# Graph attention layer on one core: feed-forward jobs of four row tiles, a pool of four PSUM banks, and a new order of steps

## The reference

```python
q, k, v = [(h @ W).reshape(n, 8, 64) for W in (Wq, Wk, Wv)]
e = einsum('ehd,ehd->eh', k[src], q[dst]) / sqrt(64)
ex = exp(e - segment_max(e, dst)[dst])
attn = ex / segment_sum(ex, dst)[dst]
a = segment_sum(attn[:, :, None] * v[src], dst).reshape(n, 512)
x1 = layernorm(h + a @ Wo, ln1_g, ln1_b)
f = relu(x1 @ W1 + b1) @ W2 + b2          # 512 -> 64 -> 512
layer = layernorm(x1 + f, ln2_g, ln2_b)
out = layernorm_plain(x + layer)          # no gain, no bias
```

## Time and profile before

| what | us |
|---|---|
| three runs | 682.5, 683.04, 686.41 |
| median | 683.04 |
| the profiled execution, first to last instruction (its span) | 682.0 |
| PE busy in it | 641.5 (94%) |
| DVE, ACT, POOL busy | 578.0, 528.3, 401.7 |

### The profile page before, as it was taken

One profiled execution on the slowest core, in us unless ns is written; L12 is line 12 of the kernel. 1 busy time (PEld: TensorE's weight loads), 2 busy tenths in 40 slices (PEclk: granted clock), 3 DMA queues, 4 the chain that ended last, 5 costly groups with the idle time before them and its releaser, 6 DMA issues. The chain is left out here.

```text
span 682.0 us, 10864 instructions
## 1 busy us (share of the span) xinstructions
PE 641.5 (94%) x3520; PEld 483.8 (71%) x3520; DVE 578.0 (85%) x1391; ACT 528.3 (77%) x1140; POOL 401.7 (59%) x363
## 2 busy tenths in 40 slices
PE   5999999999999999999999999999999999999950
PEld 2778877777777777777777777777778778675520
DVE  7668769879898898898889889988989898899792
ACT  2525269877888987988798889878878999698881
POOL 7267244867675865756776574864547726735423
PEclk9999999999999999999999999999999999999995
DMA  7844154644643745674474456455554824536452
GB/s 227 220 101 133 44 123 106 173 122 142 148 121 131 159 121 148 167 157 92 146 177 117 113 161 137 105 168 123 127 128 155 184 62 135 139 77 138 131 113 91
DMA packets 37747, 91.44 MB, mean 134 GB/s; under 512 B 8346, under 2 KB 9642, under 8 KB 37690
## 3 DMA queue, kind: packets, MB, share of 16 engines
q0 software_dynamic: 31536, 82.74, 47.6%
q1 hardware_dynamic: 6154, 8.01, 4.3%
HBM read 71.20 MB, written 20.99 MB: 135 GB/s over the span
## 5 line engine op out<-in xcount | busy, mean ns | idle before, releaser
L558 ACT ACTIVATE squares<-rows,nmean 125x512 bf16<-125x512 f32 x200 | 142.3, 713 | 41.5 <-DVE nmean L902 19.8
L412 POOL DMA_INDIRECT x_rows<-in_x_dram,node_idx x40 | 48.2, 1205 | 56.8 <-DVE rows L917 47.3
L416 POOL DMA_INDIRECT out_dram<-rows,node_idx x40 | 46.4, 1160 | 56.4 <-ACT rows L618 47.0
L473 POOL DMA_DIRECT2D x_rows<-in_L_gnn_ln_b_dram x40 | 52.9, 1372 | 31.1 <-DVE rows L821 21.7
L898 DVE SCALAR_TENSOR_TENSOR rows<-pF,rows 125x512 f32<-125x512 f32 x78 | 50.6, 686 | 23.2 <-PE pF L1103 22.5
L963 PE MATMUL pP<-wo_hi,aT_hi 128*125 128x512 f32 x160 | 65.9, 412 | 0.3 <-DVE aT_lo L848 0.3
L963 PE MATMUL pP<-xTs_hi,wv_hi 128*128 128x500 f32 x160 | 65.8, 411 | 0.0
L963 PE MATMUL pP<-xTd_hi,wq_hi 128*128 128x500 f32 x160 | 65.4, 409 | 0.1
L963 PE MATMUL pP<-xTs_hi,wk_hi 128*128 128x500 f32 x160 | 63.5, 397 | 0.6 <-ACT q L539 0.6
L963 PE MATMUL pP<-wo_lo,aT_hi 128*125 128x512 f32 x160 | 63.1, 394 | 0.0
L963 PE MATMUL pP<-wo_hi,aT_lo 128*125 128x512 f32 x160 | 63.0, 394 | 0.0
(11 more groups left out here) (197 smaller groups left out, 1760.6 us busy)
## 6 DMA issues: line engine op xcount, KB each, us to landing
x_rows<-in_L_gnn_ln_b_dram POOLq DMA_DIRECT2D x40, 512.0 KB, 6.7
dst_row<-in_dst_dram SPq DMA_DIRECT2D x9, 250.5 KB
q<-in_L_gnn_Wq_dram SPq DMA_DIRECT2D x1, 1024.0 KB, 5.6
rows<-in_L_gnn_Wk_dram SPq DMA_DIRECT2D x1, 1024.0 KB, 7.8
rows<-in_L_gnn_Wv_dram SPq DMA_DIRECT2D x1, 1024.0 KB, 6.8
x_rows<-in_L_gnn_Wo_dram SPq DMA_DIRECT2D x8, 128.0 KB, 6.0
xd<-in_x_dram,dst_idx POOLq DMA_INDIRECT x40, 4.6
xs<-in_x_dram,src_idx POOLq DMA_INDIRECT x40, 3.8
```

Of the source, the lines that this page charges most:

```text
L412: pool.indirect_dma_start(rows, None, x, bass.IndirectOffsetOnAxis(ap=table[:, column:column + 1].bitcast(U32), axis=0), bounds_check=N - ...
L416: pool.indirect_dma_start(out, bass.IndirectOffsetOnAxis(ap=table[:, column:column + 1].bitcast(U32), axis=0), rows, None, bounds_check=N ...
L473: pool.dma_start(xr_wide[n], bass.AP(tensor=be2.tensor, offset=be2.offset, ap=[[0, P], [0, 2], [1, D]]), accum_op=ALU.add).then_inc(s[f"be ...
L558: ins = act.activation(squares[:, t, :], w[n][:, t, :], ACT.Square, bias=nmean[c][n][:, t:t + 1], accum_out=sq[c][n][:, t:t + 1])
```

## The change

1. **PSUM.** Four banks pF hold only F2, row tile t in pF[t % 4]. Four banks pB hold everything else: the transposes, T, S, Q, K, V, O and F1. A string of digits, BANKS, gives each such step in PE's order its bank, and a step waits until the reader of the bank's last tenant has read it (`bank_free`, which now knows eight kinds of tenant).
2. **Feed-forward jobs of four tiles.** N0 with N1, and E0 with E1, share F1, relu and the small operations (m1, r1, m2, r2, m3, r3 and the square roots d1 to d3) in rounds 0 to 8; in round 9 each slot is a job of its own (SPLIT_FROM). F1 is eight matmuls of 250 columns, relu one operation of 128x250, F2 four matmuls. T becomes two steps T0 and T1 of four transposes. F1 starts its own accumulation, so the clearing by ACT is gone; each slot's two banks are seeded by ACT in one step. The special steps of the end (T9, B9, F19, F29, norm9, z9) are gone.
3. **Start.** The destination row alone is cast and transposed first (CASTD, TURND) and written to its table (TABD); then the other two. POOL's iotas for the counting (IOTB) move behind the first gathers. The Wk load waits for xd, the Wv load for xs. The low half of Wq moves ahead of the digits, three counting groups behind Q0.
4. **Destination row.** `dst_row` now shares its memory with `weight`, so the row of the next round is loaded only when the logarithm of this round has been taken.
5. **Order.** The table has an explicit time for every step in every round. FILLERS has 53 matmuls instead of 58, 24 of them ahead of O0 of round 9.

The core of the diff:

```diff
-PERIOD = 7684
-SLOT_PERIOD = {"N0": 7687, "N1": 7689}
+SPLIT_FROM = {"N": 9, "E": 9}
 PLAN = {
...
-V0 27356 105501 136738 136738 170605; O0 89451 141151 143013 157654 247834; TXD1 -186065 -14365 126120 126712 125690;
...
+TURND 279; TURN 562; OFFS 717; TURNF 866; TXD1 1194 3244 7938 13356 20768 25683 34085 38033 44554 49682; TXD0 1237 3602 7531
...
+BANKS = """
+012301230230231023102310231023102312301231023102310231023102120123021302102132013130123012301230123012302103021320132013201320123
...
+    (0, "TXD1"): 10, (0, "Q0"): 3, (9, "O0"): 24, (9, "E0.F1"): 4, (9, "E1.T0"): 4, (9, "E1.F1"): 8
...
+        pF = [ctx.enter_context(nc.psum_tensor(f"pF{n}", [P, 512], F32)) for n in range(4)]
+        pB = [ctx.enter_context(nc.psum_tensor(f"pB{n}", [P, 512], F32)) for n in range(4)]
...
+            on.wait_ge("xd_loaded", 64)
+            sp.dma_start(stage["k"], Wk.rearrange("(k p) n -> p k n", p=P)).then_inc(s["wk_loaded"], 16)
...
             for i in range(1, ROUNDS):
                 on.wait_ge("mask_eq", i)
+                on.wait_ge("log_taken", i)
                 sp.dma_start(dst_row[:, :], bass.AP(tensor=dst.tensor, offset=dst.offset + (EG * i - 1), ap=[[0, P], [1, EG + 1]]))\
...
+                    elif what == "seed":
+                        h = int(job[1])
...
+                        for t in (2 * h, 2 * h + 1):
+                            ins = act.activation(pF[t][0:R, :], bias_all[0:R, :], ACT.Copy)
...
+            def bank_free(i, step):
...
+                j, old = tenant_before[i, step]
+                if old[:3] in ("TXD", "TXS"):
+                    on.wait_ge("xd_lo" if old[2] == "D" else "xs_lo", nth("dve", old, j))
+                elif old[0] == "Q":
+                    on.wait_ge("q_saved", nth("act", old, j))
+                elif old[0] == "K":
+                    on.wait_ge("qk_part", nth("dve", old, j))
+                elif old == "S":
+                    on.wait_ge("weight_exp", j + 1)
+                elif old[0] == "V":
+                    on.wait_ge("weighted", nth("dve", f"W{old[1]}", j))
+                elif old[0] == "O":
+                    on.wait_ge("hx_done", nth("dve", f"H{old[1]}", j))
+                elif old.endswith(".F1"):
+                    on.wait_ge("h_done", nth("act", old.replace("F1", "relu"), j))
+                else:
+                    on.wait_ge("nT_done", nth("act", old, j))
...
                     elif what == "F1":
...
                         for k in range(KC):
-                            for t in range(2):
-                                ins = pe.matmul(pF[0][DFF * t:DFF * t + DFF, 0:R], w1[:, k, :], nT[:, k, R * t:R * t + R],
-                                                start=False, stop=(k == KC - 1), skip_group_check=True)
+                            by_half = nT[:, k, :].rearrange("p (h c r) -> p c h r", h=2, c=2)
+                            for c in range(2):
+                                ins = pe.matmul(bank[DFF * c:DFF * c + DFF, span(job)].rearrange("p (h r) -> p h r", r=R), w1[:, k, :],
+                                                by_half[:, c, halves(job)[0]:halves(job)[-1] + 1, :], start=(k == 0), stop=(k == KC - 1))
...
                     elif what == "F2":
...
-                        for t in range(2):
-                            pe.matmul(pF[1 - t][0:R, :], hT[DFF * t:DFF * t + DFF, :], w2[DFF * t:DFF * t + DFF, :],
-                                      start=False, stop=True, skip_group_check=True).then_inc(s["f_filled"], 1)
+                        for h in halves(job):
+                            for c in range(2):
+                                pe.matmul(pF[2 * h + c][0:R, :], hT[DFF * c:DFF * c + DFF, R * h:R * h + R], w2[DFF * c:DFF * c + DFF, :],
+                                          start=False, stop=True, skip_group_check=True).then_inc(s["f_filled"], 1)
```

More of the change, by code:

```diff
@@ L291, in graph_attention @@
-        turns = [(i, step, half) for i, step in pe_steps if step[:2] == "TX" or step.endswith((".T", ".T9"))
-                 for half in range(1 if step[:2] == "TX" else 2)]
-        turn = {key: n for n, key in enumerate(turns)}
-        products = [(i, step) for i, step in pe_steps if "." not in step and step[0] in "QKVO" and step[1:].isdigit()]
-        place = {key: n for n, key in enumerate(products)}
-        jobs = [(i, step.split(".")[0]) for i, step in pe_steps if step.endswith((".F1", ".F19"))]
@@ L330, in nth, with last_of @@
[L330 to L331 removed]
+            for i, step in steps[engine]:
+                done[family(step)] = done.get(family(step), 0) + (len(halves(step.split(".")[0])) if "." in step else 1)
+                numbers[engine, step, i] = done[family(step)]
+        def nth(engine, step, i):
+            return numbers[engine, step, i] if i >= 0 else 0
+        def last_of(engine, prefix, i):
+            return max(nth(engine, f"{prefix}{k}", i) for k in range(4))
@@ new lines, in graph_attention, with job_before, span, columns @@
+        jobs = [(i, step.split(".")[0]) for i, step in steps["pe"] if step.endswith(".F1")]
+        def job_before(i, job, h):
+            earlier = [old for old in jobs[:jobs.index((i, job))] if h in halves(old[1])]
+            return earlier[-1] if earlier else None
+        def span(job):
+            return slice(R * halves(job)[0], R * (halves(job)[-1] + 1))
+        def columns(job):
+            first = 4 if job[0] == "E" else 0
+            return slice(first + 2 * halves(job)[0], first + 2 * halves(job)[-1] + 2)
@@ new lines, in _ @@
+                    job, what = step.split(".")
+                    if what in ("T0", "T1"):
+                        e = int(what[1])
+                        on.wait_ge("n1_done", nth("act", f"{job}.norm", i))
+                        for c in range(2):
+                            for n, t in enumerate(rows_of(job)):
+                                ins = pe.transpose(bank[:, 2 * R * c + R * n:2 * R * c + R * n + R],
+                                                   w_rows[:, t, P * (2 * e + c):P * (2 * e + c) + P], ident[0:R, 0:R])
+                        ins.then_inc(s["turned"], 1)
```

821 lines of the change are left out of this document (367 added, 454 removed).

## The result

The changed kernel takes 706.98 us (median of four runs, 705.19 to 711.05), the kernel before beside it on the same chip 684.18. The ratio is 1.035, interval 1.033 to 1.038. The forecast was 666.6. The profiled execution has a span of 705.4 against 682.0.

The account below looks back on a forecast made before the run. The prediction took PE, 94% busy, to bound the kernel. Start -3.5, changes of kind -7.5, wider product -1, bank waits +1.8, round 9 hole 0, tail -6.2 summed to -16.4: 666.6 us, with 656 to 683 for 8 in 10.

Parts of the forecast that it names:

- the sum's steady stretch: Rounds 1 to 9 without their ends: saved ACT and DVE work beside PE gains nothing; bank waits add 1.8 us.
- rival H: From the experiments: the remaining mid-run idle time is ACT and DVE order around the norm, or the four shared banks.
- theory E: From the experiments: POOL's queue is bound by its order; issues pile up behind the stall, delaying scatters and node gathers.
- The zero for the destination row: Each round's later destination-row load costs 0; wholly uncovered, up to 6.7 us a round.
- Rival B: Pool of four banks starves PE at K-T-S-V and TX groups: 29 us of waits, about 694; chance 0.08 with B2.
- The sign set for B: PE idling over 2 us a round before a transpose, S or V with a DVE or ACT releaser.
- Rival B2: Gaps of 3 us a round lower PE's clock in the steady stretch: some 700 us; chance 0.08 with B.
- Changes of kind: On PE, fewer entries into products and feed-forward products from another kind: -7.5 us, from -5 to -9.
- the wider product: F1 of four-tile jobs, eight matmuls on 250 columns instead of twice eight on 125: -1 us, from 0 to -3.3.
- The start's marker: First xd gather at about 4.1 us and Q0 at 16 to 17.5; the start's term was -3.5, from -5 to 0.
- what the prediction called the risk: At the start, ACT's in-order weight splits could make K0 pay for the delayed Wk load; term's bound 0.
- The tail's marker: Last O to last row in 23 to 27 us; the tail's term was -6.2, from 0 to -12.4.

Follow-up runs that it names:

- e5: Changed kernel with POOL's four list gathers of rounds 3 to 9 moved ahead of its stall; 691.80 us, 1.011 of the kernel before.
- e7: Changed kernel with four unused iotas on POOL ahead of each round's list gathers, 15.1 us in all; 725.08 us, 1.059 of the kernel before.
- e9: The kernel before with the same four unused POOL iotas a round as e7; 683.84 us, ratio 1.0006.
- e6: e5 with the source gathers of rounds 3 to 9 moved behind the edge scatters and node gathers; 727.33 us, 1.064 of the kernel before.
- e8: e6 with SP asking for Wk at once behind Wq; 727.15 us, 1.063 of the kernel before.
- e10: Changed kernel with the weight splits of V and O moved behind work that doesn't wait for their loads; 714.29 us, 1.045 of the kernel before.
- e11: e5 with the moved weight splits of e10; 691.73 us, 1.013 of the kernel before.
- e13: Changed kernel with one bias addition for a job's four tiles instead of two, rounds 0 to 8; 713.23 us, 1.044 of the kernel before.
- e15: e14 with the joint bias additions of e13; 689.64 us, 1.009 of the kernel before.
- e16: e5 with the edits of e10, e3 and e13 (moved splits, Wk first, joint bias additions); 693.51 us, 1.015 of the kernel before.
- e2: Changed kernel with two-tile jobs in all rounds, first edge slot's steps earlier, a pair's F1 sharing a bank; 725.34 us, 1.059 of the kernel before.
- e14: e5 with e3's edit (list gathers in the stall, Wk behind Wq), without moved splits; 685.37 us, 1.003 of the kernel before.
- e3: Changed kernel with SP asking for Wk right behind Wq, without waiting for xd; 706.24 us, 1.033 of the kernel before.
- e4: Changed kernel with eleven constant matmuls ahead of the first edge transposes of rounds 1 to 5; 705.55 us, 1.033 of the kernel before.

## Why the prediction was wrong

**The step that failed is the sum's steady stretch.** The prediction asked there which engines lie beside PE, named DVE and ACT, and took their saved work as "slack for the new order's waits"; the waits it weighed were for banks (+1.8) and for the destination row (0). POOL stood in the same row with 343 of 561 us and was asked only about the start. The step to take would have been: POOL issues 32 DMAs a round at about 1.3 us each, some 42 of 62 us, in order; where in the new order does it stand, and what is queued behind? The count above (31 issues in 43 us behind stalls of 11 and 6) is what was missing. PE's idle time in the middle rose by 22.2 us against the 1.8 in the sum. e5, e7 and e9 show POOL's part: the same kernel takes 15 us less, with 12.7 us less idle time of PE in the middle, by the place of 28 issues; 15 us of POOL work cost 18, and cost nothing in the kernel before. So some 13 of the 22 are shown to be POOL's order; the other 9 stay open (rival H), and the forecasts from theory E failed in e6, e8, e10, e11, e13, e15 and e16. Why the new table leaves the stall there (jobs of four tiles finish more rows at once, or only the table's times) isn't separated; e2 says that narrow jobs in the new order keep it. The zero for the destination row held on DVE: from round 1 on it is never idle for more than 0.02 us before the mask that reads the row. In rounds 2 and 7, though, the mask starts 0.02 us behind the row's landing (127.4 and 455.4 us) and could not have stood earlier, and POOL waits for it there (14.7 and 10.6 us): whether the shared memory forced a late place of the mask on the table is not tested.

**Rival B** named the right sign, and came nearest to the height (694), but mostly by another mechanism, so by luck. In the changed kernel the waits for a bank's reader are 7.0 of the 25.0 us, far under its 29; 2.3 of them are for an H that itself waited 3.0 for a scatter. They are also four times the 1.8 of the sum. The sign set for B, over 2 us a round before a transpose, S or V with DVE or ACT as releaser, shows (14.5 + 2.3 + 0.8 + 1.2 in eight rounds), but most of it is T waiting for the norm and not for a bank: the sign didn't tell the two apart. Rival B2's mechanism came as a companion: gaps of 2.4 to 3.3 us, and 0.83 of the full clock in the 10 us behind one. The Trainium skill, TensorE: Matmul & The Clock Gate, A second HAM failure mode: psum-queue depth-cycling, tells of a kernel in which cycling through PSUM banks left PE briefly idle so often that its clock swung. Here the rings of four banks cycle through 100 to 600 us at a mean of 1.00 in e14 and 0.99 in the changed kernel, and the falls there are those behind the four gaps.

**Changes of kind and the wider product came out in the size forecast; two other parts of PE's work were not in these terms.** -7.5 and -1 were forecast. Counted from each matmul's start to the next, idle time left out, products, F1 and F2 take 7.7 us less in the changed kernel, 6.3 in e5 and 9.5 in e14. PE's work as a whole is 3.1, 8.0 and 9.9 less, and that these agree with 8.5 in e5 and e14 is in part luck. The bias matmuls of round 9 are gone in all three, 5.5 us:

```profile
L1072 PE MATMUL pF<-bias_all,ident 125*125 125x512 f32 x8 | 3.9, 605 | 0.0
...
L1072 PE MATMUL pP<-bias_all,ident 125*125 125x512 f32 x4 | 1.9, 593 | 0.0
```

(The lines count each to its own end.) Against this, the transposes take 8.4 us more in the changed kernel, 3.8 in e5 and 4.9 in e14; in the changed kernel those of T, which stand first behind the gaps, come every 0.125 us instead of every 0.110. A full F1 took 1.85 us, as forecast (1.8 to 2.0):

```profile
61.29 1.92 PE L1069 MATMUL pB<-nT,w 128*64 128x250 f32 x16
63.14 0.50 PE L967 MATMUL pB<-xTs_hi,wv_hi 128*128 128x500 f32 x1
```

Inside this run a pair of records starts every 0.212 us, 106 ns a record; 1.85 / 16 is 116 because the first pair takes 0.266 and the last one 0.309 until the product behind it. The prediction's 62 and 265 ns hold the ends of their runs in the same way: inside the runs, a record of 125 columns takes 53 ns in the kernel before, one of 512 takes 215 in the changed kernel. The Trainium skill's rule that the prediction set against its rows (TensorE: Matmul & The Clock Gate, Back-to-back issue gap) gives 55, 107 and 216, so the trace agrees with it inside a run, and the prediction was wrong to see the 512 columns against it. The -5 worked out from it was still too much: F1 as a whole takes 3.0 us less, since the ends of the runs stay.

**The start's marker was right, its term wrong.** The first gather issues at 4.61 (forecast 4.1) and Q0 starts at 16.34 (16 to 17.5), 4.6 earlier than the earlier trace rows:

```profile
4.61 1.22 POOL L400 DMA_INDIRECT xd<-in_x_dram,dst_idx  x1 [1.11 <-DVE dst_idx L670]
```
```profile
16.34 0.47 PE L967 MATMUL pB<-xTd_hi,wq_hi 128*128 128x500 f32 x1 [0.45 <-DVE xTd_lo L771]
...
36.91 0.58 PE L1017 MATMUL pF<-att,nT 125*125 125x1 f32 x2 [5.38 <-DVE att L752]
...
43.66 0.48 PE L967 MATMUL pB<-xTs_hi,wk_hi 128*128 128x500 f32 x1
```

K0 starts 8 us later. This is what the prediction called the risk and bounded at a gain of nothing: ACT splits the weights in order and waits for each load (0 to 60 us):

```profile
ACT wv_hi L514 <- DMA rows<-in_L_gnn_Wv_dram: 6.2, 1, 6.2
...
ACT wo_hi L517 <- DMA x_rows<-in_L_gnn_Wo_dram: 5.7, 1, 5.7
...
ACT wk_hi L514 <- DMA rows<-in_L_gnn_Wk_dram: 5.0, 1, 5.0
```

e10 brings K0 back by 8.1 us with the place of two splits, e3 by 3.7 with the place of the Wk load. The gap of 5.38 us has a second price: from 34.6 to 41.4 us the granted clock is 0.50. PE's idle time before 60 us was to fall by 3.5 and rose by 4.4. Even in e14 it is 0.5 above that of before. A first product that comes early is no gain while the products behind it wait for loads.

**The tail's marker was right, and its gain was work, not idle time.** From the last O to the last row it takes 22.6 us (671.2 to 693.8; 23 to 27 forecast, 31.2 before):

```profile
692.25 1.52 ACT L628 ACTIVATE rows<-rows,shift,rs 125x512 f32<-125x512 f32 x2 [0.43 <-DVE shift L932]
```

The stretch from the last O to the end, in the kernel before and after (columns as in the earlier trace rows):

```profile
639.20:682.04 42.84, 16.07 (x103) 8.25 (x101) 27.66 (x81) 24.54 (x61) 14.13 (x13) 0.78 0.36 97
```
```profile
671.20:705.43 34.23, 10.08 (x72) 5.36 (x72) 13.31 (x37) 16.93 (x39) 7.27 (x7) 0.72 0.29 74
```

It is 8.6 us shorter. 6.0 of these are PE work: the bias matmuls are gone (5.5) and 3.2 of T, F1 and F2 now stand ahead of the last O, against 2.6 more of fillers. Idle time falls by 2.6 there, but rises by 2.5 between 600 us and the last O, so PE's idle time at the end as a whole is 28.0 us, before 28.1. The term was -6.2; as idle time it gave 0.1, and only the bias matmuls, which its chain named, were a real gain. The hole in round 9 is 17.4 us long (642.4 to 659.8) against 16.2, within the range given.

The terms, forecast and measured, in us: start -3.5, idle time +4.4; changes of kind and the wider product -8.5, measured -7.7; waits in the middle +1.8, idle time +22.2, of which some 13 by POOL's order; tail -6.2, measured -5.5 of bias matmuls and -0.1 of idle time. Not in the sum: +10.1 for slower transposes, fillers, S and the start's small matmuls. Forecast -16.4, measured 23.4.

## What to carry to other kernels

An engine that shows as idle 44% of its time can still set the pace if it issues in order: look at its longest unbroken run of issues and at what is ready behind each of its waits, not at its share. Test it with a harmless filler of known length in both kernels: where it costs nothing the queue has slack at that place, where it costs its full length, it's on the path. And a gain at a marker (the first product, the last row) counts only if the idle time of the bound engine falls by as much over the whole stage.

## What was not expected of the hardware

- An indirect DMA of 125 rows holds POOL for 1.0 to 1.3 us in the mean (100 to 600 us of the changed kernel: gathers of edge rows 1.32, the others 1.01 to 1.14) and 0.30 to the next, so 31 of them are 43 us; a bias addition of four tiles takes as long to issue as one of two (1.463).
- The granted clock fell to 0.50 behind four single gaps of 2.4 to 3.1 us in an engine that is busy 95% of the stretch, and not behind one of 3.27. Filling them (e4) left one such fall and saved under 2 us.
